# Values' product behind the even step's unit, and another order at the front and in the last batch, in a fused attention, memory and FFN kernel on one core

## The reference

```
x = x + attn_a(layernorm(x))   # 4 batches x 512 tokens x 256, 16 heads of 16
x = x + ffn(layernorm(x))      # hidden 1024, silu(gate) * up, Hadamard transform, down
x = x + attn_b(layernorm(x))   # gated memory, decay 0.95, along the tokens
x = x + ffn(layernorm(x))

attn_a: Q, K, V = x @ Wq.T + bq, x @ Wk.T + bk, x @ Wv.T + bv
        softmax(Q K^T / 4) V, then @ Wo.T + bo
ffn:    fwht(silu(x @ W1.T) * (x @ W3.T)) @ W2.T
```

## Time and profile before

| what | value |
| --- | --- |
| median of 3 runs | 585.02 us (582.75 to 587.06) |
| the profiled execution, its own time | 586.45 us |
| its span in the trace | 584.7 us |
| TensorE's mean granted clock over the span | 0.991 |
| attention steps, from the first kq score (38.16 us) to the last values' product (252.54 us) | 214.4 us |

### The profile page before, as it was taken

The page is one execution under the profiler, slowest core; times in us unless marked ns, Lnnn a source line. Parts: engine busy times, 40 slices in busy tenths (PEclk is TensorE's granted clock), DMA queues, the critical chain, the costliest instruction groups (busy, mean ns, idle before and its releaser), DMA issues.

```text
span 584.7 us, 8896 instructions
## 1 busy us (share of the span) xinstructions
PE 564.5 (97%) x3274; PEld 389.8 (67%) x3274; DVE 380.5 (65%) x730; ACT 304.8 (52%) x559; POOL 179.1 (31%) x207
## 2 busy tenths in 40 slices
PE   7999999999999987999999999999999999999997
PEld 4553343344335433368988888898777888888887
DVE  6787898888888896745453544558887436344333
ACT  2657878867886886752334232344445233424221
POOL 4351456552545397820101010014333010101000
PEclk9988999999999999999999999999999999999999
DMA  5246530330034130020000000000000010010101
GB/s 153 63 124 231 158 118 2 111 109 3 20 113 132 55 127 3 3 72 2 1 0 1 1 1 2 1 0 1 1 1 1 0 37 1 0 37 2 36 1 37
DMA packets 17995, 25.74 MB, mean 44 GB/s; under 512 B 3048, under 2 KB 11240, under 8 KB 17568
## 3 DMA queue, kind: packets, MB, share of 16 engines
q1 hardware_dynamic: 16768, 24.11, 12.6%
q10 hardware_dynamic: 1184, 1.05, 0.6%
HBM read 10.89 MB, written 5.24 MB: 28 GB/s over the span
## 4 chain that ended last, share of the span: by engine, by line
PE 82%; ACT 5%; POOL 4%; DVE 3%; SPq 2%; issue 2%; DMA 1%; DVEq 0%; POOLq 0%; ACTq 0%
PE PS L369 79%; PE PS L380 2%; POOL xTl L1253 1%; ACT xf L774 1%; DVE PR L1222 1%; ACT PR L890 1%; ACT qf L788 1%; ACT xTh L774 1%; DVE XNs L1007 1%; ACT PR L953 1%; DMA ring<-mT 1%; POOL xf L1301 1%; DVE mxr L1026 1%; POOL XNs L1302 1%; SPq L258 1%
## 5 line engine op out<-in xcount | busy, mean ns | idle before, releaser
L369 PE MATMUL PS<-xTh,ring 128*128 128x512 f32 x608 | 188.7, 392 | 0.0
L1026 DVE TENSOR_REDUCE mxr<-PS 128x1 f32<-128x512 f32 x256 | 163.1, 681 | 30.7 <-PE PS L369 30.1
L890 ACT ACTIVATE PR<-PS 128x512 f32<-128x512 f32 x256 | 138.5, 602 | 41.6 <-PE PS L369 41.5
L369 PEld LDWEIGHTS PS<-xTh,ring 128*128 128x128 f32 x608 | 113.2, 188 | 23.6 <-issue 1.7
L369 PE MATMUL PS<-xTl,ring 128*128 128x512 f32 x304 | 110.3, 391 | 0.4 <-POOL xTl L1253 0.4
L369 PE MATMUL PS<-ring 48*128 48x512 f32 (+1 forms) x512 | 101.3, 456 | 6.2 <-DVE mxr L1026 4.4
L1171 DVE TENSOR_TENSOR PR<-PR,PS 128x512 f32<-128x512 f32 x64 | 43.8, 684 | 90.7 <-PE PS L369 71.0
L369 PEld LDWEIGHTS PS<-ring 50*128 50x128 f32 (+1 forms) x512 | 42.1, 187 | 85.1 <-ACT PR L890 57.2
L774 ACT ACTIVATE AOh<-PR 128x512 fp32r<-128x512 f32 x72 | 45.5, 632 | 101.8 <-DVE PR L1171 89.8
L1253 POOL TENSOR_TENSOR xTl<-xf,xTh 128x512 fp32r<-128x512 f32 x30 | 43.3, 1457 | 138.3 <-ACT xTh L774 138.3
L1018 DVE TENSOR_TENSOR AOl<-PR,AOh 128x512 fp32r<-128x512 f32 x72 | 51.1, 710 | 50.3 <-ACT AOh L774 50.3
(11 more groups left out here) (135 smaller groups left out, 629.8 us busy)
## 6 DMA issues: line engine op xcount, KB each, us to landing
ring<-qh SPq DMA_DIRECT2D x48, 128.0 KB, 2.7
ring<-ql SPq DMA_DIRECT2D x24, 128.0 KB, 2.7
ring<-weight_scratch SPq DMA_DIRECT2D x3, 1024.0 KB, 4.9
weight_scratch<-in_w SPq DMA_DIRECT2D x2, 1024.0 KB, 6.7
X<-in_x SPq DMA_DIRECT2D x3, 512.0 KB, 6.6
out<-X SPq DMA_DIRECT2D x6, 256.0 KB, 2.2
ring<-AOh SPq DMA_DIRECT2D x8, 128.0 KB, 2.7
ring<-AOl SPq DMA_DIRECT2D x4, 128.0 KB, 2.7
```

The source lines that it names most:

```text
L369: return nc.tensor.matmul(dst, lhsT, rhs, start=start, stop=stop, skip_group_check=True)
L890: nc.scalar.activation(PR[:, j % 8, :], PS[:, kq_bank(j), :], ACT.Exp, scale=HD ** -0.5)\
L1026: nc.vector.tensor_reduce(mxr[:, S % 2, blk, TT * p + t:TT * p + t + 1], PS[:, QK0 + i % 3, :], AX.X, ALU.max, negate=True).then_inc(max_d ...
```

## The change

It does five things.

1. `weigh_values` is called after every even step K from 2 on, with a = K / 2 - 1, behind what `shared_bank` issues there. The last one, a = 63, stays where it was.
2. At the front, the eight matmuls with xTh of stacks 0 and 1 come first, then the four with the left-over xTl. DVE makes xTl before the small product sbm, and two of the second batch's four statistics come after `stack_rows`. ACT runs `stack_hi(1)` before `weights_hi(1)`.
3. The first rows of maxima are issued on ACT's queue, right behind mT, and not on SP's behind the ring loads. Behind front steps 10 and 12 TensorE gets one more matmul whose result nobody reads (`keep_busy`, 384 columns).
4. In the last batch the first two Hadamard products stand behind steps 16 and 17 (before 14 and 16), and POOL's left-over of the output operand (`output_lo(2 * b)`) at step 13 (before 6).
5. The four left-overs of the weights W3 are made by DVE, not by POOL.

```diff
-HAD_AT = (14, 16, 26, 28)
+HAD_AT = (16, 17, 26, 28)
...
             ring_load(0, 2)
-            ring_load(0, 3, (0,))
-            max_rows(0)
-            ring_load(0, 3, (1,))
+            ring_load(0, 3)
...
+            pe.wait_ge(x_hi, 2)
+            for i in range(2):
+                pe.wait_ge(swlo_done, i + 1)
+                project_stack(i, False)
+            pe.wait_ge(x_lo, 2)
+            for i in range(2):
+                project_stack(i, True)
...
+                else:
+                    keep_busy(1, PS[:, 0, :], FILL)
...
-                if K % 2 and K >= 3:
-                    weigh_values((K - 3) // 2)
+                if K % 2 == 0 and K:
+                    weigh_values(K // 2 - 1)
...
             stack_hi(0)
+            stack_hi(1)
             weights_hi(1)
-            stack_hi(1)
...
             max_evacuate(0, OB)
+            act.wait_ge(mt_ready, 1)
+            for blk in range(2):
+                act.dma_start(*max_copy(0, blk)).then_inc(mrow_in, DMA)
...
+            for dt in range(KD):
+                dve.wait_ge(x_hi, dt + 1)
+                lo(xTl[:, 0, dt, :], PS[:, dt, :], xTh[:, 0, dt, :]).then_inc(x_lo, 1)
             dve.wait_ge(mask_done, 1)
             dve.wait_ge(sbias_in, 8 * DMA)
             nc.vector.tensor_tensor(sbm[:, :, :], ...
...
-            for t in range(TT):
+            for t in range(2):
+                tile_statistics(TT + t, TT + t)
+            stack_rows(0)
+            stack_rows(1)
+            for t in range(2, TT):
                 last = tile_statistics(TT + t, TT + t)
...
+                if w == W_LIN:
+                    dve.wait_ge(lhi_done, 4 * w + i + 1)
+                    lo(raw, raw.bitcast(F32), h).then_inc(lin_done, 1)
...
-                if s == 6 and b:
+                if s == (13 if b == BATCH - 1 else 6) and b:
                     output_lo(2 * b)
...
-                if b == BATCH - 1 and SPLIT_AT <= s < SPLIT_AT + 8:
+                if b == BATCH - 1 and SPLIT_AT <= s < SPLIT_AT + 4:
```

More of the change, by code:

```diff
@@ L164, in build @@
         w_in = [sem(f"w_in{g}") for g in range(3)]
-        lhi_done, llo_done, mem_hi, mem_lo = (sem(n) for n in ("lhi_done", "llo_done", "mem_hi", "mem_lo"))
+        lhi_done, llo_done, lin_done, mem_hi, mem_lo = (
+            sem(n) for n in ("lhi_done", "llo_done", "lin_done", "mem_hi", "mem_lo"))
         g_ready, u_ready, sg_done, hf_done, hh_done, hl_done, y_ready = (
@@ L240, in rest_rows, with max_copy @@
                     for r in zip(*(rows(qk, part, blk) for blk in range(2))) for blk, r in enumerate(r)]
+        def max_copy(S, blk):
+            b, g = S // GROUPS, S % GROUPS
+            r = HALF * blk + MROW
+            return ring[r:r + 2, b % 2, QI, 2 * g:2 * g + 2, :].bitcast(F32), mT[16 * blk:16 * blk + 16, :]
         block = ctx.enter_context(nc.Block())
@@ L274, in _, with ring_load @@
                                  AOf[0:2, :].unsqueeze(1).broadcast_to([2, PAIRS - p, SEQ])).then_inc(ones_in, DMA)
-            def ring_load(b, n, parts_=range(2)):
-                for part in parts_:
+            def ring_load(b, n):
+                for part in range(2):
                     sp.wait_ge((qk_hi, qk_lo)[part], 4 * b + n + 1)
@@ L282, in max_rows @@
             def max_rows(S):
-                b, g = S // GROUPS, S % GROUPS
                 sp.wait_ge(mt_ready, S + 1)
                 for blk in range(2):
-                    r = HALF * blk + MROW
-                    sp.dma_start(ring[r:r + 2, b % 2, QI, 2 * g:2 * g + 2, :].bitcast(F32),
-                                 mT[16 * blk:16 * blk + 16, :]).then_inc(mrow_in, DMA)
+                    sp.dma_start(*max_copy(S, blk)).then_inc(mrow_in, DMA)
             def weights_in(w):
@@ L399, in project_qk, with project_rows, project_stack, project_rest @@
                     last.then_inc(qk_ready, 1)
-            def project_rows(weights, bank, first):
-                ops = [(1, 1, 0), (0, 1, 0), (1, 1, 1), (0, 1, 1), (0, 0, 0), (0, 0, 1)]
+            def project_rows(weights, bank, left):
+                ops = [(0, 0, 0), (0, 0, 1)] if left else [(1, 1, 0), (0, 1, 0), (1, 1, 1), (0, 1, 1)]
                 for i, (lo, r, kt) in enumerate(ops):
[L405 to L409, removed]
+                    last = mm(PS[:, bank, :], weights(lo, kt), xt(0, kt)[r], i == 0 and not left, i == 1 and left)
                 return last
-            def project_stack(i):
+            def project_stack(i, left):
                 p, w = i // 2, i % 2
-                project_rows(lambda lo, kt: stack_weights(lo, w)[:, kt, p * P:(p + 1) * P], STACK_BANK[i], i == 0)\
-                    .then_inc(stk_ready, 1)
+                last = project_rows(lambda lo, kt: stack_weights(lo, w)[:, kt, p * P:(p + 1) * P], STACK_BANK[i], left)
+                if left:
+                    last.then_inc(stk_ready, 1)
+            def project_rest(left):
+                last = project_rows(lambda lo, kt: rest_weights(lo)[:, kt, :], REST_BANK, left)
+                if left:
+                    last.then_inc(qk_ready, 2)
             def project_v(b, half, part, bank=MB):
@@ L508, in _ @@
             pe.wait_ge(pad_done, 1)
[L509 to L512, removed]
+            pe.wait_ge(x_hi, 2)
[5 more added lines that the diff above has]
+                project_stack(i, True)
             pe.wait_ge(rwlo_done, 1)
-            project_rows(lambda lo, kt: rest_weights(lo)[:, kt, :], REST_BANK, False).then_inc(qk_ready, 2)
+            for left in (False, True):
+                project_rest(left)
             def beside_maxima(U):
                 if U < 2:
-                    project_stack(2 + U)
+                    for left in (False, True):
+                        project_stack(2 + U, left)
                 elif U < 6:
@@ L758, in memory_phase @@
                 return lambda: load_out(BATCH - 1, 1)
-            pe.wait_ge(llo_done, 8)
+            pe.wait_ge(llo_done, 4)
+            pe.wait_ge(lin_done, 4)
             pe.wait_ge(w2l_done, FT // 2)
@@ L1056, in _ @@
                                     ALU.mult).then_inc(sbm_done, 1)
-            for dt in range(KD):
-                dve.wait_ge(x_hi, dt + 1)
-                lo(xTl[:, 0, dt, :], PS[:, dt, :], xTh[:, 0, dt, :]).then_inc(x_lo, 1)
             def stack_rows(i):
@@ L1067, in _ @@
             dve.wait_ge(x_in[1], DMA)
-            for t in range(TT):
+            for t in range(2):
[3 more added lines that the diff above has]
+            for t in range(2, TT):
                 last = tile_statistics(TT + t, TT + t)
             last.then_inc(bst_done, 1)
-            stack_rows(0)
-            stack_rows(1)
             moments(TT, TT, 2)
@@ L1425, in _ @@
                     add_bo(b)
-                if b == BATCH - 1 and SPLIT_AT <= s < SPLIT_AT + 8:
+                if b == BATCH - 1 and SPLIT_AT <= s < SPLIT_AT + 4:
                     n = s - SPLIT_AT
                     pool.wait_ge(lhi_done, n + 1)
-                    h, raw = quarter(n // 4, n % 4)
+                    h, raw = quarter(W_UP, n)
                     lo(raw, raw.bitcast(F32), h).then_inc(llo_done, 1)
```

## The result

The changed kernel takes **603.62 us** (median of 4 runs, 603.38 to 604.09). The kernel before took 584.55 us in the same comparison (4 runs, 582.75 to 587.06). The ratio is **1.0296, 95% interval 1.0261 to 1.0332**: slower by 3%. The profiled execution took 604.09 us with a span of 602.3 us, 17.6 more than the span of before.

The account below looks back on a forecast made before the run. TensorE's own program bounds attention with scores in fours, DVE's three banks with eights. From 586.45 us: -2.3 - 0.5 - 3.2 + 0.5 + 12.2 + 0.2 + 0.6 - 0.2 + 1.8 = +9.1, so 595.6 us; range 581 to 601.

Parts of the forecast that it names:

- the main term: Step pairs behind step 7, batches 0 to 3: eight scores in a row wait for a row maximum, 0.45 us each, +12.2.
- The maxima's transfer comes nearer to its use ... nothing: Attention steps: the first pair needing the transfer stands ahead of the one waiting for DVE anyway; no cost if SP is free.
- The 11 pairs with a transpose of maxima: Pairs whose odd step has that transpose: it falls into the new wait, 3.65 to 3.73 against 3.70 us, together +0.2.
- W3's left-overs. Nothing either way: Last batch: four instructions of about 0.7 us each move to DVE where it has no row maxima; no effect, otherwise 2.8.
- The three waits for the bank of the values: Batch 0 step 18, last batch steps 2 and 10: the product waits 0.8 us, less 0.2; +0.6 in batch 0.
- The last batch to step 18: The 2.61 us wait ahead of the Hadamard product goes, but bank waits, eights and step 18's output projection return it: -0.2.
- The tail's +1.8: End of last batch: the last transpose of maxima comes about 2 us later, its transfer 1.5; +1.8 us (0 to 2.5).
- The clock: Behind the first kq score: with TensorE's wait filled, the granted clock stays up over 40 to 47 us, gaining 3.2.
- The first row maximum: Front: left-overs ready earlier, so DVE reaches its first row maximum at about 16.7 instead of 19.0, gaining 2.3 us.
- The clock falls all the same: Rival: the clock still drops once TensorE waits at the front; +3.2 us, 598.8 us in all; chance 0.2.
- The wait is absorbed: Rival: TensorE had slack at the fourth pair, so pairs stay at 3.23 us; about 583 us in all; chance 0.2.
- Fewer changes of kind win: Rival: no wait at the fourth pair, eights save some 0.25 us a pair, 6.8 in all; 576 us; chance 0.1.

Follow-up runs that it names:

- the first experiment's kernel: The changed kernel with only the values' product put back behind odd steps: 582.06 us, ratio 0.9947 to the kernel before.
- the fourth's: The kernel before with only the last batch's parts (Hadamard products at 16 and 17, output left-over at 13, W3's left-overs on DVE): 585.79 us, ratio 0.9979.

## Why the prediction was wrong in size and right in kind

The forecast was 595.6 us with a range to 601. Slower, by the named mechanism, was right; the time was 8 us off, and outside the range of 581 to 601.

**The step that failed** is the main term, "27 x 0.45 = 12.2 us". It measured 16.0. Both its factors were too small. There are 31 such pairs, not 27: in batch 0 those at steps 8, 10, 14, 16, 26 and 30, in batches 1 and 2 twelve each, in batch 3 one. The count of 27 was too short for the places where projections, output projections and input transposes stand. That is 1.8 us. And each costs 0.50, not 0.45. Its one unknown was the step from a projection to the values' product, which I took as 0.24 to 0.27 "as both of its sides use all 128 rows". It took 0.32 to 0.33 (58.42 to 58.75), the upper bound, which was the distance from a projection to scores in the earlier trace rows. The nearest row was thus that of the change of kind, not that of the same rows. So the grouping saves nothing on changes of kind: a pair loses the wait of 0.43 and another 0.1, since the scores behind a wait take 0.43 to the next item and others 0.33. With the two pairs at step 26 costing 0.65, as there the values' product waits another 0.35 for DVE's transpose, that is 2.0 us more. The price with the bounds at their ends, 31 x 0.50, would have given 598.9 us. The rest of the miss lies in the steps that follow.

**Smaller steps that failed.** "The maxima's transfer comes nearer to its use ... nothing" was wrong: where no projection stands between, TensorE waits for it, 0.87 us at 79.70, 3.0 us in six places over the whole kernel (not all of it adds: where the wait is 0.16 to 0.31, the fourth pair still comes 1.41 after the first). The 11 pairs with a transpose of maxima cost 1.0 instead of 0.2. The transpose does fall into the wait, but the 3.70 of before held for the pairs at steps 4 and 12 alone, which lose 0.03 (3.73). Those at 28 took 3.62 and take 3.74, those at 20 took 4.33 and lose 0.11 to 0.19. "W3's left-overs. Nothing either way" was wrong by some 2 us: DVE has no row maxima there, but it has the Hadamard product's evacuation (W2h, W2l), and the new instructions stand ahead of it. They took 1.65, 0.69, 0.69 and 0.98 us, 4.0 together and not 2.8. The three waits for the bank of the values came at their places and at 0.72 to 0.73 each, near the 0.8, but the profile names the exponential as what ended them; DVE's transpose ended only about 0.14 earlier, and which of the two holds the product no run shows. The last batch to step 18 has the wait that I named (0.60 for W2h), but its stretch came out 0.6 higher than I had it. The tail's +1.8 came out as +3.3, of which 1.3 are the wait for W2l and two are waits for exponentials of 0.94 each.

**Steps that held.** The clock: 1.00 over 40 to 47, worth 2.8 us where I said 3.2. The even rule in steps 3 to 6 of the front: +0.6 for 0.5 (12.57 us from the first kq score to step 8 with values odd, 13.19 in the kernel after). The first row maximum 1.95 earlier where I said 2.3; in that execution the front itself began 0.6 later (xTh at 10.00, before 9.34), which is most of what the first kq score missed. The waits for mxr: forecast 12 us or more, measured 13.4. The wait for POOL ahead of the Hadamard product is gone.

**The rivals.** "The clock falls all the same" did not happen in the kernel after. With the values odd, it falls without the fillers, for 5 us. "The wait is absorbed" is out: the kernel with the values odd again is 21.6 us faster. "Fewer changes of kind win" is out as well: with both engines' work halved the pair is still 3.46 us. Without the 0.16 that is left of the wait and the 0.1 behind it, it would be 3.2 (an estimate from these rows), about the 3.23 of before and not 0.25 less: the step from a projection to the values' product costs as much as one next to scores. Of the ten runs of eight before, seven were at 1.40 to 1.41 and three at 1.57 to 1.58, not eight and two; it changes nothing in the sum.

The Trainium skill (Perfetto Trace Analysis, Optimization Strategy) reads the same gap repeating on the engine that should be saturated as a sign that there may be too few buffers. The trace agrees as far as it goes: TensorE waits 35 times for a row maximum, 13.4 us together, each time for one of three banks. No run here gave the scores a fourth bank, and in this program all eight have a use. Beside weight loading, the Trainium skill (Perfetto Trace Analysis, Identifying the Most-Contended Engine) also names MFU, the share of the peak FLOP/s; the prediction left that out.

## What to carry to other kernels

An order that groups items of one kind looks as if it saved changes of kind on TensorE; here it saved none. And a run of items that all need the same small ring of banks stops where the ring ends, here at the fourth pair of three banks; look for the longest such run already in the program, price one, and then count the new ones in the listed order of instructions, not in the loop's conditions. Where a new sequence has no row in the trace, take the upper of its two bounds into the forecast if the change repeats it dozens of times. And before work is moved to an engine "with nothing to do there", list what that engine still owes the critical one in that stretch.

## What the runs showed of the hardware

The spread of the kernel before, 580.9 to 592.6 us, goes with TensorE's mean clock, which fell at two places of the front, and two matmuls whose result nobody reads hold it at one of them: without them 585.5 to 590.5 us, with them 581.3 to 583.1 (the first experiment's kernel). A wait of 1.77 us was followed by half clock, one of 0.51 was not; one of 1.47 was so in the profiled execution of the first experiment's kernel (clock 0.86 over 239 to 244),

```profile
242.27 1.82 PE L372 MATMUL PS<-XNs,had 128*128 128x512 f32 x2 [1.47 <-DVE W2l L1175]
```

and was not in the fourth's (1.12 us for the same product behind the same 1.47, at 241.87). So the length of the wait alone does not decide.

DVE's left-over pass over 128x512 took 1.65 us where it is 0.69 elsewhere (DVE and POOL, kernel after):

```profile
250.62 4.50 DVE L1132 CAST ring<-ring 128x512 fp32r<-128x512 f32 x4
252.02 4.23 POOL L1274 TENSOR_TENSOR ring<-ring 128x512 fp32r<-128x512 f32 x3 [0.36 <-DVE ring L1132]
255.15 1.65 DVE L1034 TENSOR_TENSOR ring<-ring 128x512 fp32r<-128x512 f32 x1
256.72 0.41 DVE L1132 CAST ring<-ring 128x512 fp32r<-128x512 f32 x1
257.17 0.69 DVE L1034 TENSOR_TENSOR ring<-ring 128x512 fp32r<-128x512 f32 x1
```

The slow one runs beside POOL's own left-overs, which end at 256.25. Of the four casts ahead of it the last two, each beside them all the way, took 1.50 and 1.49; the cast behind their end took 0.41. The first left-over is as slow (1.65 to 1.66) in all seven kernels here that have it, and in the kernel with W3's left-overs on POOL again, where POOL works on, a third cast in a row is slow as well (1.50). That points at POOL as the neighbour. No run took POOL's work away, and why the two hold each other up stays open.
